# A routed expert FFN at the end of a ViT block: leftover hidden units weighted on GpSimd before one shared output product, on one Trainium2 core

## The reference, cut

```python
x    = rmsnorm(h5) * ln2_w                       # 1024 tokens x 64
p    = softmax(x @ router_w.T)                   # 8 experts
val, idx = top_k(p, 2)                           # the first of equals wins
w    = val / (sum(val) + 1e-9)
for e in range(8):                               # 170 hidden units each
    y_e = (silu(x @ w1[e].T) * (x @ w3[e].T)) @ w2[e].T
out  = layernorm(h4 + h5 + sum_e w[token, e] * y_e)
```

## Time and profile before

| what | us |
|---|---|
| median of 3 runs (134.49 to 134.5) | 134.5 |
| the profiled execution's own time | 134.5 |
| its span, first to last instruction | 132.7 |
| PE / DVE / ACT / POOL busy in the span | 119.8 / 85.7 / 65.0 / 21.0 |
| the unit loop, by PE | 85.2 to 106.4 |
| the tail after it, by PE | 106.4 to 127.2 |
| last normalisation and store | 127.2 to 132.7 |

### The profile page before, as it was taken

How to read it: one execution, slowest core, us unless ns; L and a number is a source line. 1 busy time by engine, 2 the same in 40 slices (tenths; PEclk the granted TensorE clock), 3 DMA queues, 4 the chain that set the end, 5 groups by cost and what they waited for, 6 DMA issues and landing times.

```text
span 132.7 us, 2382 instructions
## 1 busy us (share of the span) xinstructions
PE 119.8 (90%) x928; PEld 76.9 (58%) x935; DVE 85.7 (65%) x192; ACT 65.0 (49%) x126; POOL 21.0 (16%) x26
## 2 busy tenths in 40 slices
PE   6998999789999799999999999799999999999620
PEld 2343566556778557865777876588888734323300
DVE  0000798899991494758885535767789885189980
ACT  4001668953333484367628375846666650433240
POOL 7300029000000000000250000009992000000000
PEclk9999999999999999999999999999999999999995
DMA  4999960000000000000000000000000000000003
GB/s 167 367 401 443 408 252 0 0 0 0 5 0 2 5 0 2 0 5 0 0 0 5 0 0 5 0 0 0 0 0 0 0 7 0 0 0 0 0 0 79
DMA packets 2682, 7.15 MB, mean 54 GB/s; under 512 B 1264, under 2 KB 1392, under 8 KB 2544
## 3 DMA queue, kind: packets, MB, share of 16 engines
q1 hardware_dynamic: 2672, 7.01, 13.7%
HBM read 6.75 MB, written 0.26 MB: 53 GB/s over the span
## 4 chain that ended last, share of the span: by engine, by line
PE 68%; DVE 14%; DMA 7%; issue 4%; ACT 3%; SPq 2%; DVEq 0%; ACTq 0%
PE PS L606 8%; PE PS L607 8%; PE PS L616 7%; DMA shared_x<-x_dram 7%; PE PS L390 5%; PE PS L304 4%; PE PS L510 3%; PE PS L376 3%; PE PS L293 3%; PE PS L367 3%; PE PS L492 3%; DVE shared_x L1235 3%; PE PS L312 2%; PE PS L533 2%; SPq L249 2%
## 5 line engine op out<-in xcount | busy, mean ns | idle before, releaser
L606 PE MATMUL PS<-xf,up_hi 128*128 128x512 f32 x44 | 17.3, 394 | 0.5 <-DVE xf L1141 0.5
L1202 DVE TENSOR_TENSOR shared_h<-PS,shared_f 128x512 f32<-128x512 f32 x22 | 15.1, 690 | 4.1 <-ACT shared_f L826 3.7
L607 PE MATMUL PS<-xf,up_lo 128*128 128x512 f32 x44 | 17.1, 390 | 0.0
L826 ACT ACTIVATE shared_f<-PS 128x512 f32<-128x512 f32 x22 | 13.2, 598 | 7.8 <-PE PS L607 7.8
L274 PE MATMUL PS<-idle_bf 128*128 128x512 bf16 x46 | 13.7, 420 | 1.8 <-POOL idle_bf L846 1.3
L616 PE MATMUL PS<-shared_h,down_w 128*64 128x512 f32 (+1 forms) x72 | 15.1, 553 | 0.0
L891 POOL TENSOR_TENSOR r_exp<-euler,r_shift 128x64 f32<-128x64 f32 x1 | 10.6, 10594 | 20.8 <-DVE r_shift L1214 20.8
L674 ACT ACT_TABLE_LOAD x8 | 10.3, 1283 | 0.8 <-PEq L1361 0.7
L1005 DVE TENSOR_REDUCE top<-PS 128x8 f32<-128x512 f32 x12 | 8.3, 689 | 3.2 <-PE PS L510 1.7
L274 PEld LDWEIGHTS PS<-idle_bf 128*128 128x128 bf16 x53 | 5.2, 105 | 8.7 <-issue 4.2
L606 PEld LDWEIGHTS PS<-xf,up_hi 128*128 128x128 f32 x44 | 8.3, 188 | 2.4 <-DVE xf L1141 0.8
(11 more groups left out here) (183 smaller groups left out, 206.8 us busy)
## 6 DMA issues: line engine op xcount, KB each, us to landing
shared_x<-x_dram SPq DMA_DIRECT2D x6, 544.0 KB, 6.6
up_w<-pack_d_dram SPq DMA_DIRECT2D x1, 1408.0 KB, 12.2
pack_c_sb<-pack_c_dram SPq DMA_DIRECT2D x1, 787.5 KB, 12.9
down_w<-pack_e_dram SPq DMA_DIRECT2D x1, 512.0 KB, 13.6
pack_b_sb<-pack_b_dram SPq DMA_DIRECT2D x1, 455.0 KB, 9.3
out_dram<-normed SPq DMA_DIRECT2D x4, 64.0 KB, 1.7
pack_a_sb<-pack_a_dram SPq DMA_DIRECT2D x1, 162.0 KB, 8.7
```

The source lines that it names most:

```text
L606: mm(PS[:, UP_BANKS[n % UPBUF] + v, :], up_hi[:, at:at + P], xf[:, s, :], start=True, stop=False)
L607: t = mm(PS[:, UP_BANKS[n % UPBUF] + v, :], up_lo[:, at:at + P], xf[:, s, :], start=False, stop=True)
L826: f(gate[:, n % UPBUF, :], PS[:, UP_BANKS[n % UPBUF], :], ACT.Silu).then_inc(sem("gated"), 1)
L1202: v.tensor_tensor(hh[:, ch, s, :], PS[:, UP_BANKS[n % UPBUF] + 1, :], gate[:, n % UPBUF, :], ALU.mult)\
```

## The change

1. **Output product.** `expert_down` keeps the two matmuls over the expert's own 128 units. The leftover units of all eight experts are multiplied by their weights first, in SBUF, by GpSimd; then `rests_down` runs one product over chunks 0 to 2 with a shared `down_w` block, in two token halves of 256 columns.
2. **Weights over partitions.** The turned weights get 16 unsplit rows more. ACT copies them to `whole_rows`, SP writes them to DRAM (16 rows of 2 KB), waits, and reads each expert's two rows back in a broadcast over 42 partitions: eight reads, 172 KB each.
3. **Routing in the loop.** The steps are rewritten: the exponential as a quotient of two `Silu` values on ACT, four subtractions or products on GpSimd, the others on DVE behind units 0 to 14. `routes_to_rows` stands before unit 17 on PE, the two copies behind units 16 and 17 on ACT. The sums and centring of `h45` move from behind units 9 and 13 to behind 15 and 19.
4. **End.** Expert 7 goes whole. PE writes `h45` into the final banks by a product with the identity and adds `total6` to it as matmuls; DVE no longer adds `h45`, and ACT and the scaling read PSUM.

```diff
@@ sync @@
+            sp.wait_ge(sem("whole_rows_made"), 1)
+            sp.dma_start(scratch, whole_rows[2 * 2 * NE:3 * 2 * NE, :]).then_inc(sem("routes_kept"), 16)
+            sp.wait_ge(sem("routes_kept"), 16)
+            for ex in range(NE):
+                ch, n = ex // PER_REST, ex % PER_REST
+                sp.dma_start(rest_w[ch][n * REST:(n + 1) * REST, :].rearrange("q (s c) -> q s c", s=2),
+                             scratch.rearrange("(s e) c -> e s c", s=2)[ex].unsqueeze(0).to_broadcast([REST, 2, COLS]))\
+                    .then_inc(sem(f"rest_w_loaded{ch}"), 16)
@@ tensor: before unit n of the loop @@
+                if n == ROUTE_TURN:
+                    routes_to_rows()
@@ tensor: the tail @@
+            def rests_down(g):
+                pe.wait_ge(sem("expert_weighted"), 3 + g)
+                tok = slice(g * HC, (g + 1) * HC)
+                for ch in range(RESTS):
+                    pe.wait_ge(sem("rest_weighted"), 2 * ch + 2)
                     for s in range(2):
-                        r = slice(HALF * s, HALF * s + HALF)
-                        t = mm(PS[r, bank, tok], down_w[:, at:at + D], hh[:, ch, s, tok],
-                               start=(ch == RESTS + e), stop=(ch < RESTS))
+                        t = mm(PS[HALF * s:HALF * s + HALF, REST_BANKS[g], tok], down_w[:, DOWN_AT[ch]:DOWN_AT[ch] + D], hh[:, ch, s, tok],
+                               start=(ch == 0), stop=(ch == RESTS - 1))
+                t.then_inc(sem("rest_mm"), 1)
...
             expert_down(0, DOWN_BANKS[0], every)
-            expert_down(1, DOWN_BANKS[1], every)
             pe.wait_ge(sem("hh_ready"), 2 * CH)
-            expert_down(2, DOWN_BANKS[2], every)
-            routes_to_rows()
-            expert_down(3, DOWN_BANKS[3], every)
             spread_routes(0)
             spread_routes(1)
-            expert_down(4, DOWN_BANKS[4], every)
+            expert_down(1, DOWN_BANKS[1], every)
+            expert_down(2, DOWN_BANKS[2], every)
...
+            expert_down(7, DOWN_BANKS[7], every)
+            pe.wait_ge(sem("h45_centred"), 1)
+            for g in range(2):
+                pe.wait_ge(sem("expert_weighted"), 5 + g)
+                mm(PS[:, FINAL_BANKS[g], 0:HC], ident, half(h45, g), start=True, stop=True, skip_group_check=True)
+            rests_down(0)
+            rests_down(1)
             for g in range(2):
                 pe.wait_ge(sem("total6_ready"), g + 1)
                 for u in (2 * g, 2 * g + 1):
-                    t = tp(PS[:, FINAL_BANKS[g], (u % 2) * P:(u % 2 + 1) * P], total6[:, u * P:(u + 1) * P], ident)
-                t.then_inc(sem("total6_turned"), 1)
+                    t = mm(PS[:, FINAL_BANKS[g], (u % 2) * P:(u % 2 + 1) * P], total6[:, u * P:(u + 1) * P], ident,
+                           start=False, stop=True, skip_group_check=True)
+                t.then_inc(sem("h6_ready"), 1)
@@ scalar: behind Silu of unit n @@
+                if n == 2:
+                    act.wait_ge(sem("logits_read"), 1)
+                    f(small["silu_plus"][:, :, :], small["shift"][:, :, :], ACT.Silu, scale=-1.0, bias=const(1.0))\
+                        .then_inc(sem("router_silu"), 1)
+                if n == 3:
+                    f(small["silu_minus"][:, :, :], small["shift"][:, :, :], ACT.Silu, bias=const(-1.0))\
+                        .then_inc(sem("router_silu"), 1)
+                if n == ROUTE_TURN - 1:
+                    act.wait_ge(sem("routes_turned"), 1)
+                    f(whole_rows[4 * NE:6 * NE, :], PS[4 * NE:6 * NE, ROUTED_BANK, :], ACT.Copy).then_inc(sem("whole_rows_made"), 1)
+                if n == ROUTE_TURN:
+                    f(route_rows[:, :], PS[0:4 * NE, ROUTED_BANK, :], ACT.Copy).then_inc(sem("route_rows_made"), 1)
@@ gpsimd @@
-            g_.tensor_tensor(small["exp"][:, :, :], euler[:, :, :], small["shift"][:, :, :], ALU.pow).then_inc(sem("router_exp"), 1)
+            routed, helped = sem("router_step"), sem("router_help")
+            pool.wait_ge(routed, 3)
+            pair("below1", "rank1", spread("first_rank"), ALU.subtract).then_inc(helped, 1)
...
+            for ch in range(RESTS):
+                used = REST * len(experts_of(ch))
+                pool.wait_ge(sem("hh_ready"), 2 * ch + 2)
+                pool.wait_ge(sem(f"rest_w_loaded{ch}"), 16 * len(experts_of(ch)))
+                for s in range(2):
+                    g_.tensor_tensor(hh[0:used, ch, s, :], hh[0:used, ch, s, :], rest_w[ch][0:used, s * COLS:(s + 1) * COLS], ALU.mult)\
+                        .then_inc(sem("rest_weighted"), 1)
@@ vector @@
+                if n == 3:
+                    ve.wait_ge(sem("router_silu"), 1)
+                    v.reciprocal(small["over_plus"][:, :, :], small["silu_plus"][:, :, :]).then_inc(sem("over_made"), 1)
...
+                if n == 5:
+                    ve.wait_ge(routed, 4)
+                    ve.wait_ge(helped, 1)
+                    v.scalar_tensor_tensor(out=small["others"][:, :, :], in0=small["below1"][:, :, :], scalar=0.0,
+                                           in1=small["exp"][:, :, :], op0=ALU.is_lt, op1=ALU.mult).then_inc(routed, 1)
...
+                if n == 14:
+                    ve.wait_ge(routed, 15)
+                    v.tensor_tensor(route_parts[:, :, 1, :], routes, route_parts[:, :, 0, :], ALU.subtract)\
+                        .then_inc(sem("route_split"), 1)
-            for e in range(NE - 1):
+            for e in range(NE):
                 ve.wait_ge(sem("down_mm"), e + 1)
                 ve.wait_ge(sem("routes_out"), e + 1)
                 v.tensor_tensor(product[:, e], PS[:, DOWN_BANKS[e], :], spread_w[:, e % 4], ALU.mult)\
...
+            ve.wait_ge(sem("experts_summed"), NE - 1)
+            for g in range(2):
+                ve.wait_ge(sem("rest_mm"), g + 1)
+                v.tensor_tensor(half(total6, g), half(PS[:, REST_BANKS[g], :], g), half(summed, g), ALU.add)\
                     .then_inc(sem("total6_ready"), 1)
```

More of the change, by code:

```diff
@@ L53, in experts_of @@
     return range(chunk - RESTS, chunk - RESTS + 1)
-DOWN_AT = [D * sum(len(experts_of(ch)) for ch in range(n)) for n in range(CH + 1)]
+DOWN_AT = [D * n for n in range(CH + 1)]
 EPS = 1e-5
@@ L197, in build @@
         small = {k: sb("r_" + k, [P, 8, NE]) for k in
-                 ("low", "logits", "shift", "exp", "prob", "same1", "rank1", "one1", "prob2", "same2", "rank2", "one2",
-                  "part1", "part2", "both", "weights")}
+                 ("logits", "shift", "silu_minus", "silu_plus", "over_plus", "exp", "rank1", "below1", "others", "less", "rank2", "below2",
+                  "below", "chosen")}
         few = {k: sb("r_" + k, [P, 8]) for k in
-               ("top", "sum", "rsum", "first", "first_rank", "second", "second_rank", "total", "total_eps", "rtotal")}
-        route_parts = sb("route_parts", [P, 4, 2, 2 * NE])
+               ("top", "sum", "first_rank", "second", "second_rank", "total", "total_eps", "rtotal")}
+        route_parts = sb("route_parts", [P, 4, 3, 2 * NE])
+        whole_rows = sb("whole_rows", [HALF, COLS])
+        rest_w = [shared_x[:, (NE + 2 * ch) * COLS:(NE + 2 * ch + 2) * COLS] for ch in range(2)]
+        rest_w.append(q_groups[:, :, :, :].rearrange("q w h n -> q (w h n)"))
         route_rows = sb("route_rows", [4 * NE, COLS], F32R)
@@ L591, in router_products, with routes_to_rows @@
                 t.then_inc(sem("logits_mm"), 1)
+            def routes_to_rows():
+                pe.wait_ge(sem("route_split"), 1)
+                for u in range(4):
+                    t = mm(PS[0:6 * NE, ROUTED_BANK, u * P:(u + 1) * P], route_parts[:, u].rearrange("q l k -> q (l k)"), ident,
+                           start=True, stop=True)
+                t.then_inc(sem("routes_turned"), 1)
             pe.wait_ge(sem("xf_ready0"), 2)
@@ L838, in _ @@
                 act.wait_ge(sem("h6_ready"), g + 1)
-                f(half(squares, g), half(h6, g), ACT.Square).then_inc(sem("lnf_squared"), 1)
+                f(half(squares, g), PS[:, FINAL_BANKS[g], 0:HC], ACT.Square).then_inc(sem("lnf_squared"), 1)
             roots("lnf", std, 1.0 / D, EPS)
@@ L888, in _, with pair, spread @@
                 .then_inc(sem("masks_made"), 1)
-            pool.wait_ge(sem("consts_made"), 2)
-            pool.wait_ge(sem("logits_read"), 1)
-            g_.tensor_tensor(small["exp"][:, :, :], euler[:, :, :], small["shift"][:, :, :], ALU.pow).then_inc(sem("router_exp"), 1)
+            def pair(dst, x0, x1, op):
+                return g_.tensor_tensor(small[dst][:, :, :], small[x0][:, :, :], x1, op)
+            def spread(name):
+                return few[name][:, :].unsqueeze(2).to_broadcast([P, 8, NE])
+            routed, helped = sem("router_step"), sem("router_help")
+            pool.wait_ge(routed, 3)
+            pair("below1", "rank1", spread("first_rank"), ALU.subtract).then_inc(helped, 1)
+            pool.wait_ge(routed, 6)
```

(59 more changed lines are left out.)

86 lines of the change are left out of this document (35 added, 51 removed).

## The result

Four runs of the changed kernel took 130.44 to 131.49 us, median 131.14, against 134.5 before: a ratio of 0.9736, 95% interval 0.9713 to 0.976. The forecast was 130.9. The profiled execution took 131.49, at the top of its runs, with a span of 129.7.

A forecast was written before the change was run, and what follows sets the result against it. Bound: a late start of DVE's weighting plus DVE's chain, with PE's output products lying under both. 134.5 - 4.9 (weighting hidden) + 1.3 (DVE and GpSimd interfering) = 130.9 us; range 129.4 to 132.7.

The forecast's parts named there:

- The loop takes the routing at no cost: Unit loop: routing steps cost PE 0, units stay at 0.906; only the turning's 0.99 moves in, loop ends at 107.4.
- DVE starts 6.0 earlier: Start of the tail: DVE begins weighting at 109.7 instead of 115.72.
- Both halves are needed: Tail: cutting output products alone would gain little, because DVE's late start at 115.72 has to move too.
- The time with the weighting hidden, 129.6: Whole kernel: with the rests' weighting wholly hidden, 134.5 - 4.9 = 129.6.
- The transfers: Weights through DRAM: write lands in 1.7, eight reads take about 7, first chunk at 109 to 110, last at 113.
- GpSimd's product, 1.3: Leftover units' weighting: each GpSimd product of 512 columns takes 1.3, six take 7.8 and end at 118.
- The two engines in each other's way: Tail, DVE additions beside GpSimd products: 0 to 3.9 on DVE's chain, middle 1.95 taken, 1.35 at the end.
- rival 3: Tail: full exclusion of DVE additions and GpSimd products, delay 3.1 to 3.9, time 132.1 to 132.9; chance 0.15.
- case 1: Tail: DVE and GpSimd partly in each other's way, the forecast itself, 130.9 (130.0 to 132.0); chance 0.45.
- The products hidden by 1.6 us: Tail: GpSimd's six products end at 118, PE asks for the last at 119.6, so PE doesn't wait.

## Why the prediction was right, step by step

- **The loop takes the routing at no cost.** Right: units stayed at 0.906 but for the turning, and `route_split` came at 101.20 where I had 101.3. The loop ended 0.3 later than forecast; 0.07 of it was there at the loop's start, and 0.2 lies in the first matmul after the turning (0.43). I had priced every small step alike; the slack of three units swallowed the reciprocal of 0.54.
- **DVE starts 6.0 earlier.** Measured 109.97 against 115.72, 5.75; the forecast was 109.7.
- **Both halves are needed.** Shown for one of them. I said that products alone gain little and that the start has to move. The other half, that an early start alone gains nothing since PE's eight full products take until 125.0, was the expectation of the routing-only run, and it came but for 0.35%: 134.2, and PE's part ended at 124.96. That products alone gain little stays an argument from the earlier trace rows, not run.
- **The time with the weighting hidden, 129.6.** The run without the weighting gave 129.84, the one with sums from PSUM 129.93.
- **The transfers.** The write landed in 1.6 (forecast 1.7). The eight reads ran at 184 to 227 GB/s between 106.2 and 112.2, half of the 421 of the earlier trace rows, which made them end near 113 as forecast. But the first chunk had landed only at 111.7, two us after my 109 to 110.

Stretches of the changed kernel, columns as in the earlier trace rows:

```profile
108.20:109.20 1.00, 1.00 (x6) 0.29 (x2) 0.40 (x1) 0.99 (x2) 0.00 (x0) 1.00 0.88 205
...
112.20:113.20 1.00, 1.00 (x8) 0.29 (x4) 0.76 (x2) 0.59 (x2) 1.00 (x2) 1.00 0.41 100
```

- **GpSimd's product, 1.3.** Undisturbed 1.27 or 1.28; beside the additions the step was 1.68.
- **The two engines in each other's way.** Here the time was right partly by luck. The forecast took the middle between no effect and exclusion, 1.95 us on DVE's chain and 1.35 at the end. Measured on the chain: 1.09 + 4 x 0.36 = 2.5. At the end the profiled executions with and without the weighting lie 1.68 apart (last squaring at 124.67 and 122.99), but the first is its kernel's slowest; the ratios give 1.1 to 1.2. What happened is the mechanism of rival 3, one instruction waiting for the other, at a time of case 1. The row that spoke for no effect, the centring at 0.68 under the end of GpSimd's power, didn't carry over: beside a product of 512 columns it took 1.35. Rival 3's price was too high for two reasons. A pair of DVE instructions grows by 0.36 (1.68 - 1.32), not 0.65: whole instructions taking turns would need 1.27 + 0.69 = 1.96 a round, so about 0.3 of the two still overlaps, and which part wasn't shown. And DVE had more room before PE's end than the 0.6 that I gave it: without the weighting its last addition ended at 120.41 and PE's rests at 121.72, which, with 1.71 from that addition to the squaring in the changed kernel, leaves 0.9. So 130.9 came out because two errors, too mild a mechanism and too dear a unit price, met.
- **The products hidden by 1.6 us.** Wrong in the changed kernel: later transfers and products of 1.7 made POOL end at 121.08, and PE waited 0.49. This wait was not on the chain that ended last, which was DVE's until 123.43.

The Trainium skill (SBUF — State Buffer, "Who interferes with whom") says that the second of the two to issue blocks until the first is done. The traces agree in kind: 1.35 for a centring of 0.68, 1.78 for an addition of 0.69 behind a product of 1.27. They differ in degree: a round took 1.68 and not 1.96, and beside GpSimd's multiplication by a constant two additions weren't held up at all. The measurement decides. The same section says that a DVE instruction with at most one SBUF input, outside the two-port performance modes, doesn't contend with GpSimd; the multiplications' 0.69 and the run with sums from PSUM bear that out.

## What to carry to other kernels

Before work goes to GpSimd beside a busy DVE, count the DVE instructions in that stretch with both operands in SBUF: they and GpSimd's took turns here, at 1.09 us for the first addition and 0.36 for each later one. Leaving an intermediate in its PSUM bank for the next DVE instruction took them out of each other's way and cost DVE nothing. When two engines are both close behind the bound, moving one of them alone gives next to nothing (134.2 against 134.62); after each move look again at which engine owns the chain, since an edit that saves PE time for DVE's pays only once PE is the bound (the old end: nothing before the exclusion was gone, 0.7 us after).

## What the runs showed of the hardware that I had not expected

- Of the chain's 0.94 of "issue" between two DVE multiplications, 0.37 was a DVE addition blocked by GpSimd. The profile names no releaser for such a block; what gives it away is one instruction's length, 1.05 against 0.69, with another engine in step.
- GpSimd's multiplication of 512 columns by a constant took 1.49, longer than its product of two tensors at 1.27.
- Reads issued in order didn't complete in order of the chunks: by 111.7, some 1.15 MB of 1.38 had moved (the sum of the rates from 106.2 on), more than twice the first chunk's 0.5 MB, and only then did GpSimd's wait for its third read end. In the profiled executions GpSimd started anywhere from 109.80 to 111.96. The changed kernel's runs spread over 1.05 us (130.44 to 131.49), those with sums from PSUM over 0.33 (129.74 to 130.07). That the shifting start of the products makes the difference is likely, but wasn't shown.
